# Other orders of work in four stages of a four-layer graph network kernel

## Time and profile before

| | us |
|---|---|
| median of 3 runs (lowest, highest) | 4888.4 (4885.79, 4892.55) |
| the profiled execution's own time | 4877.32 |
| its span, first to last instruction | 4875.6 |
| POOL busy | 3540.1 (73%) |
| VectorE (DVE) busy | 2974.1 (61%) |
| TensorE (PE) busy | 2345.5 (48%) |
| ScalarE (ACT) busy | 933.1 (19%) |

### The profile page before, as it was taken

The page is one execution under the profiler, slowest core; times in us unless marked ns, Lnnn a source line. Parts: engine busy times, 40 slices in busy tenths (PEclk is TensorE's granted clock), DMA queues, the critical chain, the costliest instruction groups (busy, mean ns, idle before and its releaser), DMA issues. The chain is left out here.

```text
span 4875.6 us, 30472 instructions
## 1 busy us (share of the span) xinstructions
PE 2345.5 (48%) x8870; PEld 1413.8 (29%) x8870; DVE 2974.1 (61%) x3609; ACT 933.1 (19%) x1345; POOL 3540.1 (73%) x3150
## 2 busy tenths in 40 slices
PE   7810155666477770000342223047766477775652
PEld 3400033433344440000342223012222244443331
DVE  8865066665677764666632222046666599997774
ACT  0011011111244441111000000024444111111110
POOL 8777676662777726777488888877775677777777
PEclk9955555555699995555555555568888678877776
DMA  1034234332244432222122222245543111111100
GB/s 27 10 120 143 36 87 89 82 84 63 88 145 146 145 138 74 64 78 65 32 5 5 5 5 5 5 115 159 156 151 123 32 29 29 31 27 30 27 25 9
DMA packets 348967, 327.80 MB, mean 67 GB/s; under 512 B 223275, under 2 KB 295862, under 8 KB 347596
## 3 DMA queue, kind: packets, MB, share of 16 engines
q1 hardware_dynamic: 85600, 236.67, 13.6%
q0 software_dynamic: 144256, 45.62, 9.8%
q10 hardware_dynamic: 118944, 43.56, 3.7%
HBM read 170.38 MB, written 156.58 MB: 67 GB/s over the span
## 5 line engine op out<-in xcount | busy, mean ns | idle before, releaser
L1353 POOL DMA_INDIRECT sum_table<-e_add_rows,e_add_idx x392 | 654.5, 1670 | 174.8 <-issue 118.3
L534 POOL DMA_INDIRECT d_ring<-g_table,pos x392 | 390.9, 997 | 217.4 <-issue 124.1
L534 POOL DMA_INDIRECT c_ring<-x_table,pos x392 | 397.7, 1015 | 202.5 <-issue 125.6
L534 POOL DMA_INDIRECT b_ring<-h_table,src x392 | 406.3, 1036 | 177.3 <-issue 114.7
L534 POOL DMA_INDIRECT g_ring<-x_table,pos x392 | 410.9, 1048 | 169.7 <-issue 119.1
L344 POOL DMA_INDIRECT x_dst<-in_x,dst x392 | 432.9, 1104 | 129.0 <-issue 129.0
L1889 PE MATMUL g_pX<-w,g_h_T 128*128 128x512 f32 x784 | 440.2, 712 | 173.8 <-DVEq L1746 173.8
L534 POOL DMA_INDIRECT f_ring<-con_table,pos x392 | 417.6, 1065 | 133.4 <-issue 126.5
L1709 POOL DMA_INDIRECT out_x<-g_out_rows,end_index x392 | 425.8, 1086 | 119.5 <-issue 119.5
L1618 PE MATMUL f_pH<-f_T,w2in 128*128 128x448 f32 x672 | 316.8, 617 | 274.2 <-DVE f_T L1510 274.2
L1400 PE MATMUL e_pS<-e_values,e_equal 128*128 128x17 f32 x784 | 168.6, 374 | 416.3 <-DVEq L1373 416.3
(11 more groups left out here) (342 smaller groups left out, 5248.3 us busy)
## 6 DMA issues: line engine op xcount, KB each, us to landing
f_sums<-sum_table ACTq DMA_DIRECT2D x126, 238.0 KB
sum_table<-c_zero SPq DMA_DIRECT2D x39, 715.0 KB, 5.3
g_table<-c_g SPq DMA_DIRECT2D x42, 448.0 KB, 2.4
h_table<-a_xp SPq DMA_DIRECT2D x28, 560.0 KB, 3.5
a_x<-in_x SPq DMA_DIRECT2D x28, 448.0 KB, 6.0
b_h_node<-h_table ACTq DMA_DIRECT2D x28, 448.0 KB, 4.6
b_x_node<-in_x SPq DMA_DIRECT2D x28, 448.0 KB, 3.5
x_table<-b_x_node SPq DMA_DIRECT2D x28, 448.0 KB, 2.5
```

The lines of the kernel that those rows point to most:

```text
L534: pool.indirect_dma_start(out=ring[:, t, :], out_offset=None, in_=table, in_offset=bass.IndirectOffsetOnAxis(ap=idx[:, c * C + t:c * C + t ...
L1353: pool.indirect_dma_start(out=g.sums[b], out_offset=bass.IndirectOffsetOnAxis(ap=aidx[:, c % 2, t:t + 1], axis=0), in_=add[:, c % 2, t, :] ...
```

## The change

- Tables: the 98 constants that `hot_high` compares with are copied to the free columns of `w.bank` in PSUM (`highs`), and read from there.
- Attention: VectorE's `add_x1("n", 2c+1)` moves from before `w.finish` to after `dst_scores(c + 1)`. TensorE's order per chunk changes: both `turn_back` come right after their `turn`, the projections after them.
- First message stage: `filled` and `taken` count banks, not uses; TensorE and ScalarE hand over each bank by itself, so each fill and each copy or activation is two. The copy of the mask for the next chunk moves ahead of `bring("mean", c)`; `add_r("n", 2c)` moves behind the chain; `turn_back` comes ahead of `hidden("n", 2c + 1)` in the last chunk alone.
- Adding stage: the triangle product and its reduction go. `val` gets an 18th column with a power of two that falls by half with each partition, so that TensorE's sums tell whether a lower partition has the same index; VectorE waits for them (`summed`), compares with twice its own power (`first`), and ScalarE's copy waits until that is read (`sums_read`). `eq` is double.

The diff, cut to its core:

```diff
@@ stage_tables
+        highs = w.bank[:, Norm.USED:Norm.USED + HIGH]
...
-                                        bc_tile(wide[:, 0:HIGH], C), ALU.is_equal)
+                                        bc_tile(highs, C), ALU.is_equal)
...
+            nc.vector.tensor_copy(highs, wide_i[:, 0:HIGH])
@@ stage_attention, VectorE
-                add_x1("n", 2 * c + 1)
-                if more:
                     w.finish(dve, n, hd[:, 1 - c % 2])
                     dve.drain()
                 values(c)
                 if more:
                     dst_scores(c + 1)
+                add_x1("n", 2 * c + 1)
                 sums(c)
@@ stage_attention, TensorE
-            for k in range(2):
-                quads("n", k)
-                project("n", k)
+            quads("n", 0)
+            project("n", 0)
+            quads("n", 1)
             for c in range(EC):
+                more = c + 1 < EC
                 if c:
                     quads("e", c - 1)
                 mx.turn(pe, c, most[:, C - 1:C])
-                if c:
-                    project("e", c - 1)
                 mx.turn_back(pe, c)
-                if c + 1 < EC:
-                    quads("n", 2 * c + 2)
+                project("n", 2 * c + 1)
                 pe.wait_ge(cum_ready, c + 1)
...
+                if c:
+                    project("e", c - 1)
+                if more:
+                    quads("n", 2 * c + 2)
                 pe.wait_ge(kept, c + 1)
                 nm.turn(pe, c, run[:, :, C - 1])
-                if c + 1 < EC:
+                nm.turn_back(pe, c)
+                if more:
                     project("n", 2 * c + 2)
-                nm.turn_back(pe, c)
-                if c + 1 < EC:
                     quads("n", 2 * c + 3)
-                    project("n", 2 * c + 3)
@@ stage_sage_first
+        banks = ((0, 512), (512, Q * P))
+        def at(n, h):
+
+            return 2 * (n - 1) + h + 1
@@ VectorE
-                add_r("n", 2 * c)
                 ahead = 2 * c + 2
...
                 cr.chain(dve, c, g.preall[0:F, c, :])
+                add_r("n", 2 * c)
@@ ScalarE
-                act.wait_ge(filled, use["turn", kind, k])
-                nc.scalar.copy(tsb[:, {"hd": 0, "mean": 1, "n": 2}[kind], :], pT[:, 0:Q * P]).then_inc(taken, 1)
+                for h, (lo, hi) in enumerate(banks):
+                    act.wait_ge(filled, at(use["turn", kind, k], h))
+                    nc.scalar.copy(tsb[:, {"hd": 0, "mean": 1, "n": 2}[kind], lo:hi], pT[:, lo:hi]).then_inc(taken, 1)
...
+                if more:
+                    copy_mask(c + 1)
                 bring("mean", c)
                 hidden("e", c)
@@ TensorE
-                pe_quads(nc, pT, src, g.ident[:], filled)
+                for h, (lo, hi) in enumerate(banks):
+                    if n > 1:
+                        pe.wait_ge(taken, at(n - 1, h))
+                    for q in range(lo // P, hi // P):
+                        last = nc.tensor.transpose(pT[:, q * P:(q + 1) * P], flat(src[:, 4 * q:4 * q + 4, :]), g.ident[:])
+                    last.then_inc(filled, 1)
...
                 cr.turn(pe, c, run[:, :, C - 1])
+                if c + 1 == EC:
+                    cr.turn_back(pe, c)
                 hidden("n", 2 * c + 1)
-                cr.turn_back(pe, c)
+                if c + 1 < EC:
+                    cr.turn_back(pe, c)
                 product("n", 2 * c + 1)
@@ stage_symmetric, VectorE
-                if c:
-                    dve.wait_ge(summed, c)
-                nc.vector.tensor_tensor(eq[:], pB[:].rearrange("p (t k) -> p t k", k=P), bc_feat(g.posF[:, part(c)], P), ALU.is_equal)
+                nc.vector.tensor_tensor(eq[:, a], pB[:].rearrange("p (t k) -> p t k", k=P), bc_feat(g.posF[:, part(c)], P), ALU.is_equal)
...
-                nc.vector.tensor_tensor(eqb[:], eq[:], bc_tile(g.before[:], C), ALU.mult)
...
-                nc.vector.tensor_reduce(rank[:], eqb[:], AX.X, ALU.add)
...
+                dve.wait_ge(summed, c + 1)
+                nc.vector.tensor_scalar(first[:], sums[:, :, CW], twice[:, 0:1], None, ALU.is_le)
+                dve.drain().then_inc(sums_read, 1)
+                nc.vector.tensor_tensor(shift[:], first[:], shift[:], ALU.mult)
@@ ScalarE
+                act.wait_ge(sums_read, c + 1)
+                nc.scalar.copy(add[:, c % 2], sums[:, :, 0:CW]).then_inc(add_ready, 1)
```

More of the change, by code:

```diff
@@ L986, in _ @@
                 if c:
[L987 removed]
+                    dve.wait_ge(filled, at(use["turn", "hd", c - 1], 1))
                 w.finish(dve, n1, hd[:]).then_inc(h_ready, 1)
@@ L1005, in _ @@
                 if c:
-                    dve.wait_ge(filled, use["turn", "mean", c - 1])
+                    dve.wait_ge(filled, at(use["turn", "mean", c - 1], 1))
                 cr.arrive(dve, c)
@@ L1035, in keep_g, with copy_mask @@
                 nc.scalar.copy(halves(gt[:, n % 2]), products()[:, :, :, 0:F]).then_inc(g_sb, 1)
-            w.squares_then_roots(act, 2)
-            for c in range(EC):
+            def copy_mask(c):
                 if c:
@@ L1041, in _ @@
                 nc.scalar.copy(mask[:], bc_tile(g.same0[:, part(c)], F)).then_inc(masked, 1)
+            w.squares_then_roots(act, 2)
+            copy_mask(0)
+            for c in range(EC):
                 if not c:
@@ L1075, in quads @@
                 pe.wait_ge(sem, k + 1)
-                if n > 1:
-                    pe.wait_ge(taken, n - 1)
-                pe_quads(nc, pT, src, g.ident[:], filled)
+                for h, (lo, hi) in enumerate(banks):
+                    if n > 1:
[3 more added lines that the diff above has]
+                    last.then_inc(filled, 1)
             def hidden(kind, k):
                 for r in range(2):
-                    pe.wait_ge(taken, use[f"hid{r}", kind, k] - 1)
-                    for lo, hi in ((0, 512), (512, Q * P)):
+                    for h, (lo, hi) in enumerate(banks):
+                        pe.wait_ge(taken, at(use[f"hid{r}", kind, k] - 1, h))
                         if kind == "e":
@@ L1096, in product @@
                 for r in range(2):
[L1097 to L1101, removed]
+                    for h, (lo, hi) in enumerate(banks):
+                        pe.wait_ge(taken, at(use[f"hid{r}", kind, k], h))
+                        for q in range(lo // P, hi // P):
+                            i = 2 * q + r
+                            last = nc.tensor.matmul(pG[:, i // Q, (i % Q) * P:(i % Q + 1) * P], hid[:, r, q * P:(q + 1) * P],
+                                                    g.w1gr[:], start=True, stop=True)
                 last.then_inc(gr_done, 1)
@@ L1322, in stage_symmetric @@
         SW = lambda name: g.lasting(f"e_{name}")
-        eq, eqb = sb("equal", [P, C, P]), sb("equal_before", [P, C, P])
-        val, add = sb("values", [P, 2, C, CW]), sb("add_rows", [P, 2, C, CW])
+        eq = sb("equal", [P, 2, C, P])
+        val, add = sb("values", [P, 2, C, CW + 1]), sb("add_rows", [P, 2, C, CW])
+        power_i, power, twice = sb("power_i", [P, 1], i32), sb("power", [P, 1]), sb("twice_power", [P, 1])
         aidx = sb("add_idx", [P, 2, C], i32)
-        rank, shift = sb("rank", [P, C]), sb("shift", [P, C])
+        first, shift = sb("first", [P, C]), sb("shift", [P, C])
         pB = ctx.enter_context(nc.psum_tensor("e_pB", [P, C * P], f32))
         pS = ctx.enter_context(nc.psum_tensor("e_pS", [P, 512], f32))
-        val_ready, spread, eq_ready, summed, add_ready, idx_ready = (
-            S(x) for x in ("val_ready", "spread", "eq_ready", "summed", "add_ready", "idx_ready"))
+        sums = pS[:, 0:C * (CW + 1)].rearrange("p (t w) -> p t w", w=CW + 1)
+        powers, val_ready, spread, eq_ready, summed, sums_read, add_ready, idx_ready = (
+            S(x) for x in ("powers", "val_ready", "spread", "eq_ready", "summed", "sums_read", "add_ready", "idx_ready"))
         R = len(g.sums)
@@ L1361, in _ @@
             nc.vector.memset(val[:], 1.0)
+            dve.wait_ge(powers, 1)
+            nc.vector.tensor_copy(power[:], power_i[:].bitcast(f32))
+            dve.drain()
+            nc.vector.tensor_scalar(twice[:], power[:], 2.0, None, ALU.mult)
+            for a in range(2):
+                nc.vector.tensor_copy(val[:, a, :, CW], power[:, 0:1].to_broadcast([P, C]))
             dve.drain()
@@ L1398, in _ @@
                     pe.wait_ge(add_ready, c)
+                    pe.wait_ge(sums_read, c)
                 for t in range(C):
-                    last = nc.tensor.matmul(pS[:, t * CW:(t + 1) * CW], eq[:, t, :], val[:, c % 2, t, :], start=True, stop=True)
+                    last = nc.tensor.matmul(sums[:, t, :], eq[:, c % 2, t, :], val[:, c % 2, t, :], start=True, stop=True)
                 last.then_inc(summed, 1)
@@ L1408, in _ @@
                     wait_added(act, c - 2)
-                nc.scalar.copy(add[:, c % 2].rearrange("p t w -> p (t w)"), pS[:, 0:C * CW]).then_inc(add_ready, 1)
```

(2 more changed lines are left out.)

14 lines of the change are left out of this document (6 added, 8 removed).

## The result

| | us |
|---|---|
| median before, measured beside it | 4890.48 |
| median after (lowest, highest) | 4689.38 (4685.58, 4694.78) |
| ratio | 0.9591, interval 0.9574 to 0.9607 |
| the profiled execution after, its span | 4694.78, 4693.0 |

The account below looks back on a forecast made before the run. GpSimd's indirect DMAs were taken to bound the tables and adding stages, a VectorE, ScalarE and TensorE loop attention and the first message stage. Terms -33 - 42 - 79 - 53 = -207 us gave a 4681 us median, range 4645 to 4745.

Parts of the forecast that it names:

- What binds, and what binds next: Attention and first message stage: a VectorE, ScalarE and TensorE loop binds now; POOL's gathers bind after the edit.
- Loops stay above POOL: Rival, chance 0.16: attention and message-stage loops stay slower than POOL, gaining only 60 and 25 us; 4728 us.
- Tables, -33: Tables stage: moving one comparison operand to PSUM ends the stretch of 14 gathers, 2.38 us each; -33 us.
- Adding, -42: Adding stage: removing the masked product ends the stretch of scatters, and the first chunk costs 1 us; sum -42 us.
- The adding stage turns serial: Rival, chance 0.02: the adding stage's new chain runs after the previous chunk's scatters, not under them; 4928 us.
- Attention, -79: Attention: earlier carry returns cut VectorE's loop from 44.4 to 33.7 us per chunk, so POOL binds; -79 us.
- their 392 gathers need 406.3 + 114.7 + 5 = 526 us: Attention: POOL's time for all gathers, from the profile before, taken as the floor once ring waits go.
- First message stage, -53: First message stage: bank hand-over and new orders bring VectorE's loop from 41 to about 36 us, under POOL; -53 us.
- The sum: All four changed stages: -33 - 42 - 79 - 53 = -207 us, for a median of 4681 us.
- a loop of VectorE, ScalarE and TensorE sets the pace: Attention and first message stage before the change: this loop, not POOL's gathers, was taken to bind.
- The price of the two returns: Attention: VectorE's waits for maximum and sums, some 7.4 and 5.1 us per chunk; 12.5 of 44.4 us go.

Follow-up runs that it names:

- the reductions that cost nothing in the kernel after: Kernel after plus three unread VectorE reductions of 1.09 us per attention chunk, right behind the running sums: 4676.66 us, ratio 0.9566.
- the first of the two placements in the kernel before: Kernel before plus three unread VectorE reductions of 1.09 us per attention chunk, right behind the running sums: 4889.7 us, ratio 0.9995.

## Why the prediction was right

**What binds, and what binds next** is borne out by the rows of after: no wait for a ring, and VectorE waiting for rows in both loops. *Loops stay above POOL* fell with that, and with the reductions that cost nothing in the kernel after.

**Tables, -33.** Right: 577.0 to 543.6 over all traces. In the pair of profiles POOL's busy time fell by 32.6 us (432.9 to 400.3) and 5.2 us of "issue" came back. The prediction quotes from the Trainium skill (SBUF — State Buffer, Who interferes with whom) that an operation with at most one SBUF input doesn't contend with GpSimd, without the page's condition that it be outside the 2-port perf modes, and says that there the trace agrees. That is too wide: it holds for the comparison with PSUM and the reduction of the earlier trace rows, while gathers under the one-operand comparisons of `hot_low` are stretched by 21 us here. No run shows in which mode these ran. The prediction left that stretch out of its term, so the sum doesn't suffer.

**Adding, -42.** Right, and by its mechanism: the removed product's stretch was the gain, the reduction's none. The first chunk cost nothing where 1 us was taken. *The adding stage turns serial* had its wait (11 to 12 us in each chunk) and no consequence, since the next chunk's index waits for scatters anyway.

**Attention, -79, measured -74 to -76.** VectorE's loop came to 32.8 us, predicted 33.7; the sums' return waits 0.43 us per chunk, predicted 0.4; the last chunk's tail is 3 us shorter, predicted 2. The step that was off is "their 392 gathers need 406.3 + 114.7 + 5 = 526 us": they take 531.8 us, from 545.8 to 1077.6. The difference is three gaps ahead of single gathers, 2.62, 2.50 and 2.65 us, one of them in the time line above. Before, with its waits for a ring, the stage has no such gaps: the rows of a stage in which POOL rests were taken for one in which it does not.

**First message stage, -53, measured -47 to -49.** Through the last centering -42 was predicted and -34.5 came (1654.08 in a stage that begins at 1121.8, against 1789.95 in one from 1223.2), since the gathers took 530 us, not 523: "issue" 131.0 instead of 125.6, with three gaps of 4.25 us, before 2.01, 2.04 and 3.95. VectorE comes to that centering without a wait, 1.75 us behind the end of the last gather, so its loop and the gathers end level. Behind it the tail fell by 12 us where 11 was predicted. VectorE's loop was taken as 36 us and is lower: 88.8 us of waits for rows, less the 30 that the first two chunks have in either kernel, are 4.9 us in each of the 12 others, out of a mean 37.8 us from one to the next, so about 33. It changes nothing, POOL being the floor.

**The sum.** -207 predicted, -201 measured, and -200 by the means of the stages. What the forecast missed is mainly POOL's gaps.

One sentence of the prediction is narrower than it reads. That "a loop of VectorE, ScalarE and TensorE sets the pace" was right, but the first of the two placements in the kernel before shows that VectorE's 44.4 us were not one path: work added where it waits for TensorE is free. The price of the two returns held, because it was taken from waits that TensorE ended.

## What to carry to other kernels

Where GpSimd issues indirect DMAs without pause, look at what long VectorE operations read: one operand in PSUM gave back 2.4 to 3.3 us for each here, at the same duration on VectorE. When a loop lies close above a floor, the first repair brings it to the floor and the second brings little more; take the floor's own time from a stage in which it runs without waits. Before pricing added or saved work on an engine, find which of its waits stands behind that place: the same 45.6 us of reductions cost 0 or 45.6 us on the two sides of one instruction, by whether a wait for another engine could take them in.

## What the runs showed of the hardware

**Gaps ahead of every 113th gather.** In the tables stage, attention, both message stages and the third layer POOL stands still after 113, 225 or 226, and 337 to 339 indirect DMAs of that stage, with nothing in the profile that ends it. In the kernel after it does so for 3.19, 7.15 and 4.68 us in the tables stage, 2.62, 2.50 and 2.65 in attention, 4.25 three times in the first message stage, 1.98, 1.90 and 1.92 in the second, 2.71, 2.02 and 4.58 in the third layer. The kernel before has such gaps in the same stages (3.34, 3.34 and 3.2 in the tables stage) but none in attention, where POOL waits for a ring ahead of every chunk from its 141st gather on. The five other traces with that stage as before have one, of 1.9 to 2.0 us after 113 gathers, ahead of the first such wait, and none later. The 392 scatters of the adding stage, spaced 1.85 us apart instead of 1.25, have none. That a backlog of issued DMAs has to drain would fit; no run tried it, so the cause stays open.

**One operand's place.** A product of 128 x 3584 with both operands in SBUF holds the scatter that begins under it for the product's whole rest, 4.76 us instead of 1.55; with one operand in PSUM it holds none, and VectorE takes 3.89 us for both.
